# Adding beta2 + b2 to y2's rows on GpSimd, in place of a product with ones inside ff2

## What is computed

```
y  = layernorm(y + ca, g2, beta2)                       # y2
h  = relu(einsum("bsd,df->bsf", y, w1) + b1)            # ff1, 256 -> 1024
ff = einsum("bsf,fd->bsd", h, w2) + b2                  # ff2, 1024 -> 256
y  = layernorm(y + ff, g3, beta3)
```

## Time and profile before

| | |
|---|---|
| time, median of 3 runs | 609.63 us (608.44 to 609.86) |
| the profiled execution | 611.56 us, its span 609.7 us |
| busy: PE, DVE, ACT, POOL | 565.5, 494.1, 377.9, 387.9 us |
| granted TensorE clock, mean | 0.966 of full speed |
| the chain of waits | PE 77%, POOL 7%, issue 6%, DVE 6%, ACT 2% |
| DMA | 19.30 MB, 32 GB/s on average |

### The profile page before, as it was taken

How to read it: one execution, slowest core, us unless ns; L and a number is a source line. 1 busy time by engine, 2 the same in 40 slices (tenths; PEclk the granted TensorE clock), 3 DMA queues, 4 the chain that set the end, 5 groups by cost and what they waited for, 6 DMA issues and landing times.

```text
span 609.7 us, 12399 instructions
## 1 busy us (share of the span) xinstructions
PE 565.5 (93%) x4021; PEld 539.0 (88%) x4021; DVE 494.1 (81%) x1211; ACT 377.9 (62%) x781; POOL 387.9 (64%) x466
## 2 busy tenths in 40 slices
PE   4788589999999999999999999999999999999675
PEld 3687589999999999999999999999999999988665
DVE  4997868888888888887988888888888888787752
ACT  3665376667758575766666684858666675755331
POOL 3686556686657667676767666776658666665631
PEclk9788799999999999999999999999999999999887
DMA  7701001010101001010201010000101010000000
GB/s 229 232 2 36 0 2 44 1 54 1 60 2 54 2 20 43 0 52 0 60 0 52 0 54 6 27 24 0 60 2 35 2 35 3 17 2 18 10 9 17
DMA packets 18743, 19.30 MB, mean 32 GB/s; under 512 B 1537, under 2 KB 18193, under 8 KB 18705
## 3 DMA queue, kind: packets, MB, share of 16 engines
q1 hardware_dynamic: 18704, 18.82, 10.1%
HBM read 14.62 MB, written 4.19 MB: 31 GB/s over the span
## 4 chain that ended last, share of the span: by engine, by line
PE 77%; POOL 7%; issue 6%; DVE 6%; ACT 2%; DMA 1%; SPq 0%; POOLq 0%; DVEq 0%; ACTq 0%
PE R L988 6%; PE R L990 5%; PE R L989 5%; PE TR L892 5%; PE O L1040 5%; PE R L1058 5%; PE R L1060 5%; PE R L1059 5%; PE O L1103 5%; PE O L1105 4%; PE O L1104 4%; PE R L892 4%; PE O L1082 3%; PE O L1084 3%; PE O L1083 3%
## 5 line engine op out<-in xcount | busy, mean ns | idle before, releaser
L988 PE MATMUL R<-gu_hi,xqT_hi 128*128 128x352 f32 x256 | 86.2, 337 | 3.0 <-ACT xqT_hi L659 1.2
L442 POOL TENSOR_TENSOR rs<-mv,neg_half 128x1 f32<-128x1 f32 (+1 forms) x112 | 70.6, 640 | 26.9 <-DVE mv L1363 25.6
L695 ACT ACTIVATE hqT_hi<-R 128x768 fp32r<-128x768 f32 x32 | 26.0, 813 | 97.6 <-PE R L892 97.6
L1058 PE MATMUL R<-y2T_hi,w_hi 128*128 128x256 f32 x256 | 77.8, 304 | 7.5 <-DVE y2T_lo L1491 4.6
L990 PE MATMUL R<-gu_hi,xqT_lo 128*128 128x352 f32 x256 | 82.9, 324 | 0.0
L989 PE MATMUL R<-gu_lo,xqT_hi 128*128 128x352 f32 x256 | 82.9, 324 | 0.0
L1103 PE MATMUL O<-w_hi,hT_hi 128*128 128x256 f32 x256 | 74.9, 293 | 0.0
L448 POOL TENSOR_TENSOR hs<-hh,h_rec 128x704 f32<-128x704 f32 x32 | 44.5, 1392 | 45.3 <-DVE h_rec L1399 45.3
L1059 PE MATMUL R<-y2T_lo,w_hi 128*128 128x256 f32 x256 | 73.4, 287 | 0.0
L1060 PE MATMUL R<-y2T_hi,w_lo 128*128 128x256 f32 x256 | 73.3, 286 | 0.0
L1105 PE MATMUL O<-w_hi,hT_lo 128*128 128x256 f32 x256 | 72.3, 282 | 0.0
(11 more groups left out here) (148 smaller groups left out, 1805.9 us busy)
## 6 DMA issues: line engine op xcount, KB each, us to landing
x_in<-in_x SPq DMA_DIRECT2D x16, 256.0 KB, 2.8
x_res<-in_x SPq DMA_DIRECT2D x16, 256.0 KB, 2.8
out<-x SPq DMA_DIRECT2D x32, 128.0 KB, 1.9
ctx_rows<-in_ctx SPq DMA_DIRECT2D x16, 64.0 KB, 2.5
hT<-in_L_xattn_w SPq DMA_DIRECT2D x1, 1024.0 KB, 7.1
hh<-in_L_xattn_w SPq DMA_DIRECT2D x1, 768.0 KB, 8.8
wd_raw<-in_L_ffn_w_down SPq DMA_DIRECT2D x1, 704.0 KB, 9.9
w_raw<-in_L_ffn_w_gate SPq DMA_DIRECT2D x1, 640.0 KB, 4.6
```

The costliest lines, as they stand in the source:

```text
L988: mm(o, xh, gu_hi[:, c, m, cols], start=(c == 0), stop=False)
L1058: mm(o, w1_hi[:, c, cols], y2T_hi[:, c, :], start=(c == 0), stop=False)
```

## The change

`shift_parts` is no longer filled, and the matmul with ones goes from `ff2`; the first matmul of chunk 0 now opens the sum in O[1]. In its place GpSimd adds `shift2_row` to y2's rows in place, two instructions of 128x256 a slot in a new step `y2_shift`, which stands right behind `residual`. The product with g2 (`gain_rows`) now counts in a new semaphore, y2_scaled, which `y2_shift` waits for, and y2_set, for which `ff_sum` and `cross_sum` wait on DVE, is counted by the addition. PE has 32 matmuls less, GpSimd 32 additions more; ScalarE's and VectorE's one small step each in the head are gone. The memset of `shift_parts` stays.

```
@@ -489,7 +490,12 @@
                 if norm1:
                     gain_rows(b, h, A, t, 1, z1, y1[:, t, :], g1_row, y1_set)
                 else:
-                    gain_rows(b, h, F, t, 2, z2, y2[t][:], g2_row, y2_set)
+                    gain_rows(b, h, F, t, 2, z2, y2[t][:], g2_row, y2_scaled)
+
+            def y2_shift(b, h):
+                for t in range(T):
+                    wait(pool, y2_scaled, b, h, F, T, t + 1)
+                    pool.tensor_tensor(y2[t][:], y2[t][:], shift2_row[:], ALU.add).then_inc(y2_set, 1)
 
             def slot(b, h):
                 a, f, q = live(b, h, A), live(b, h, F), live(b, h, Q)
@@ -522,6 +528,7 @@
                     masks(b, h)
                 if f:
                     residual(b, h)
+                    y2_shift(b, h)
                 if live(b, h, 0) and h == 0:
                     context_values(b)
                 if q:
@@ -598,6 +605,7 @@
                 y_rows(1, 0, True, 1)
                 pool.wait_ge(rows3_in, 16 * 2)
                 residual(1, 0)
+                y2_shift(1, 0)
                 h_lower_last(1, 0)
                 context_values(1)
                 w_scaled(4)
@@ -853,7 +861,6 @@
                 norm(2, 0, 1, A, 1, 1, z2[:, 1, :], z2[:, 1, :])
                 y2T_upper(1, 0)
                 w_abs(3)
-                shift2_upper()
                 w_upper(act, 1)
@@ -952,7 +959,7 @@
                 if isinstance(b, int) and HALVES * b + h == F:
-                    for s, n in ((w2_hi_set, 2), (w2_lo_set, 2), (shift_parts_set, 1)):
+                    for s, n in ((w2_hi_set, 2), (w2_lo_set, 2)):
                         pe.wait_ge(s, n)
@@ -1096,11 +1103,9 @@
                 o = O[1][:, 0:D]
-                if fs[0] == 0:
-                    mm(o, ones[:], shift_parts[:], start=True, stop=False)
                 for f in fs:
                     hi, lo = hT_hi[:, f, P * t:P * (t + 1)], hT_lo[:, f, P * t:P * (t + 1)]
-                    mm(o, hi, w2_hi[:, f, :], start=False, stop=False)
+                    mm(o, hi, w2_hi[:, f, :], start=(f == 0), stop=False)
                     mm(o, hi, w2_lo[:, f, :], start=False, stop=False)
@@ -1718,7 +1723,6 @@
                 w_lower(1)
-                shift2_lower()
                 w2_lower(0)
```

More of the change, by code:

```diff
@@ L225, in layer_program @@
         z2_set, y2_set = sem("z2_set"), sem("y2_set")
+        y2_scaled = sem("y2_scaled")
         n2_turned, y2T_hi_set, y2T_lo_set = sem("n2_turned"), sem("y2T_hi_set"), sem("y2T_lo_set")
```

## The result

| | median, us | runs | ratio to the kernel before, same chip (95%) |
|---|---|---|---|
| kernel before | 609.27 (608.44 to 609.86) | 6 | |
| the change | 613.69 (611.86 to 615.48) | 6 | 1.0056 [1.0030, 1.0081] |
| the change, measured again (e5) | 612.07 | 12 | 1.0045 [1.0023, 1.0066] |

The change makes the kernel some 0.5% slower, 2.7 to 3.4 us by the two ratios. The profiled execution took 614.38 us: a span of 612.4, and about 2 us around it as before.

The account below looks back on a forecast made before the run. PE was taken to set the pace, except for some 4 us of each slot where it follows chains on DVE and ACT. Terms -1.9 + 2.4 + 0 + 0.3 = +0.8 us gave 610.4 us, range 607.0 to 614.0.

Parts of the forecast that it names:

- Additions of 0.73 us, 0.69 apart: GpSimd: each addition takes 0.73 us, with 0.69 us from start to start.
- Rival 3: GpSimd: additions run at 1.28 us each if DVE's timing moves under them; +10 us, 619.6 us; chance 0.10.
- Tile 1's 0.12 us: PE, ff2 of tile 1: each removed matmul saves 0.12 us, 16 times, 1.9 us gained.
- tile 0's: PE, ff2 of tile 0: 16 removed matmuls gain 0, as PE then waits for ACT and DVE anyway.
- Slots with h = 0: Six slots: `scale_h` 0.5 us late, PE's `cross_values` and ff2 of tile 1 0.4 us later; 2.4 us lost.
- Rival 2: Slots with h = 0: `h_div` doesn't get in before `context_values`, `scale_h` 1.0 us late; +3.8 us, 613.4 us; chance 0.25.
- Slots with h = 1: Eight slots: additions fit GpSimd's 1.79 us idle time, ce 0.15 us late but hidden; 0, at most 8 x 0.1.
- The middle: All middle slots: 6 x 0.4 us lost with h = 0, less 14 x 0.12 gained, +0.7 us.
- The head, +0.3: Head: additions ahead of `h_lower_last` make it 0.5 us late, PE gets 0.22 us back; 0.3 us lost.
- the sum: Whole kernel: all gains and losses added, -1.9 + 2.4 + 0 + 0.3 = +0.8 us, 610.4 us.
- The tail, 0: Last slot with a feed-forward part: 3.41 us of idle time cover the additions; cost 0.
- "Same" at 0.50: Whole kernel: chance 0.50 of no change that a measurement can tell, within about 0.3%, 607.8 to 611.5 us.

Follow-up runs that it names:

- e5: The change itself, unaltered, measured again with more runs; 612.07 us, ratio 1.0045 to the kernel before.
- e1: Kernel before with only the matmuls with ones removed and no additions on GpSimd (beta2 + b2 left out); 608.14 us, ratio 0.9986 to the kernel before.
- e7: The change, with the head's additions behind `h_lower_last` and, in slots with h = 0, `context_values` behind it too; 612.59 us, ratio 1.0055 to the kernel before.
- e3: The change in the slots alone, the head kept as in the kernel before; 610.23 us, ratio 1.0019 to the kernel before.
- e9: Kernel before plus 141 unused filler matmuls at seven of PE's waits in head and tail; 604.78 us, ratio 0.9927 to the kernel before.
- e10: The change plus 145 unused filler matmuls at seven places in head and tail; 606.44 us, ratio 0.9959 to the kernel before.
- e12: The change with fillers, its slot additions some 3 us earlier on GpSimd, ahead of `unscale_x` of tile 1; 608.17 us, ratio 0.9980 to the kernel before.
- e11: The change with each slot's additions moved behind `scale_h` of tile 0, head as in the change; 619.17 us, ratio 1.0167 to the kernel before.

## Why the prediction was right or wrong

- **Additions of 0.73 us, 0.69 apart: right** (0.74 and 0.73, 0.71 and 0.69 apart). Rival 3 is out.
- **Tile 1's 0.12 us is gained, tile 0's not: right.** e1 shows it by itself: 5.01 unmoved, 5.83 for 5.94.
- **Slots with h = 0, `scale_h` 0.5 us late and PE 0.4: right in size** (0.47 and 0.35), half right in the way. I had `h_div` slip in between the second addition and `context_values` and push the latter. It did get in there, but as a step held from 328.12 on, and `context_values` started at 328.62 unpushed. Two paths then end almost together: GpSimd's queue lets `scale_h` start at 329.31, and `h_rec` ends at 329.17. With the first taken away (e7) the second still gives -1.20 for -1.13; the prediction had only the first. Rival 2, in which GpSimd keeps the port through both, is out.
- **Slots with h = 1: right** (`scale_h` 0.20 late for 0.15 forecast, PE's ff2 unmoved, the slot 0.13 shorter). That a slot with h = 1 should have slack and one with h = 0 none follows from 1.79 against 0.88 us of idle time.
- **The middle: 6 x 0.4 - 14 x 0.12 = +0.7 forecast, +1.22 measured** in the first profile, +1.33 in e5. The mechanism gives +0.66 of it, as forecast; the other 0.56 is PE's wait in the first slot behind the loop, for which the sum had no term.
- **The head, +0.3: right as far as it went.** The additions took 1.18 + 0.72 us (1.1 + 0.7 forecast), and PE's first ff2 started at 54.56 for 54.23. What failed is that the step ended there. TensorE's clock was low up to 60.0 instead of 56.9, about 3.1 us at 0.21 instead of 0.12 us a matmul: by 60 PE was 1.4 us late, of which 0.39 was left at the first slot. That this was the change's doing isn't shown: e3 has as long a stretch with the old head, and in e5 the first slot comes 0.4 us earlier than in the kernel before.
- **The tail, 0: 1.1 us off** in the first profile, which proves nothing. The two additions there lie under idle time, and two matmuls are gone; the clock was 0.66 for 0.77. e5, the same kernel, had 0.80 there. This part comes and goes between executions of one kernel, and with the clock held up (e9, e10) the two tails are alike to 0.1 us. The mean clock over all runs was 0.969 (6 runs) and 0.972 (12 runs) with the change against 0.974 (99 runs) without it. That fits a clock that is a little lower with the change, but the spread within a kernel is larger than the difference.

So the mechanism was right where a trace can show it, and the sum was too small: +0.8 forecast, +2.7 to +3.4 measured. With the clock held up the cost is 1.7 to 2.0 us (e9, e10), about 1 more than the sum; 0.56 of that is the wait behind the loop, the rest is not placed. The other 0.7 to 1.7 us is what a clock term would have to hold, and the sum assumed that the head and the tail take the same time whatever the clock does. "Same" at 0.50 was the likeliest case and didn't hold, at +0.5% against a bound of 0.3%. That the time lies in the range all the same is luck in part: the upper end of 614.0 was there for rival 2 (613.4), and rival 2 didn't happen.

**The shared port, after the fact.** `h_div` ended 0.04 us behind the addition's end in slots of the middle, and in e12 a step of two inputs lost 0.42 us to an addition. The Trainium skill (SBUF — State Buffer, section Who interferes with whom) says that whoever starts first keeps the shared port pair for the whole instruction; the traces agree, and add that VectorE gets in between two GpSimd instructions that follow each other without a gap.

What stays open: why PE waits behind the loop in the kernels without the matmuls; whether the change itself lowers the clock, and by how much; and a place in which the additions would cost nothing, since e11 and e12 each repaired one chain and broke another.

## What to carry to other kernels

An instruction moved to an engine with 36% idle time is free only if the idle time lies where it is put, and if no short step of VectorE on a chain runs beside it: here 0.19 us became 0.58, and each of three places on GpSimd held up another chain. Matmuls of 0.12 us that are taken away beside a wait give nothing back; e1 showed half of those here worth nothing. Before judging a difference of 0.5%, look at the clock of the windows at the start and the end, in more than one profile of each kernel, and compare the two with the clock held alike: here one pair of profiles seemed to put 1.1 us into the tail, and others took it back. And compare the distances slot by slot: 0.56 us lay at one place that the change doesn't touch.

## What the runs showed of the hardware that I had not expected

- Unused matmuls at seven places made the kernel before 0.73% faster (0.9927), at a mean granted clock of 0.991 instead of 0.966. The work added is 141 matmuls, put where PE would otherwise have stood.
- The kernel before ran from 606.9 to 612.6 us in 99 runs; e9 from 604.28 to 606.59 in 6. The spread goes with the mean clock, if not in a straight line: 607.0 us on average at 0.980 (9 runs), 609.7 at 0.978 (24), 608.5 at 0.975 (33), 611.7 at 0.969 (19).
- The two-input step of DVE and the addition held each other: 0.85 for 0.43 and 0.92 for 0.73 us (e12). A reduction of DVE under an addition (`h_max`, 0.89 us) kept its length.
- Taking away 32 matmuls brought a wait of PE of 0.44 to 0.47 us at a place where none of them stood: it is in the profiles of all nine kernels without them and in none of the five that keep some or all. Why is open.
